# First adjacency pass in five sets of blocks, weighted one-hots on ScalarE, all duplicate counts in pass zero of a four-layer graph network

## The chip, the cores and the metric

One core of one Trainium2 chip runs the whole kernel in one launch. The metric is the device time in microseconds, the median of several runs.

## The reference, cut to what matters

A graph of 6250 nodes and 106250 directed edges (100000 and a self loop per node), sorted by destination. Four residual layers, each on `relu(layernorm(x))`:

```python
edge_index = stack([src, dst])                     # 106250 edges, sorted by dst
h = relu(layernorm(x))
# L0: an edge MLP gives each edge a weight; GCN with these weights
w = sigmoid(gelu(concat(h[src], h[dst]) @ mlp_w1 + mlp_b1) @ mlp_w2 + mlp_b2)
deg = segment_sum(w with loops of 1, dst); dinv = rsqrt(deg)
x = x + segment_sum((h @ conv_w)[src] * (dinv[src] * w * dinv[dst]), dst) + conv_b
# L1: two plain GCNs (128 -> 256 -> 128), with relu
# L2: message MLP, segment_sum(m[src], dst), update MLP on concat(h, agg)
# L3: three plain GCNs of 128 x 128
```

The sums over edges of L1 to L3 need only how often each pair (src, dst) occurs; those of L0 need a weight per edge.

## The kernel before

**Preparation.** Edges are cut into 831 tiles of 128. Nodes are cut into 49 windows (as destinations; `DB` = 49) and 49 chunks (as sources) of 128. Because a tile may span two windows, the edge passes walk over 880 steps, 220 groups (`GROUPS`) of four (`S` = 4).

**Pass zero** (the edge MLP). For each group POOL gathers four times 128 rows of `table` (`gather`, L569). SP copies the rows out to `h_rows` and loads what duplicate counting needs (`load_keys`, L398). TensorE spreads the destination half, VectorE adds the halves, ScalarE does Gelu and Tanh, and VectorE splits the new weights. VectorE also does the duplicate counts, `dedupe(n)` (L1083 to L1095): for four tiles of edges it counts how often the same (src, dst) stands in the tile and clears the place of all but one. There are 208 of them (`SCATTERS`), 146 (`EARLY`) in pass zero and 62 in pass one, as `counted(p, g)` hands them out.

**Scatters.** `adj` in HBM is the matrix of counts, f16, one block of 128 destinations by 49 x 128 sources for each window. Once POOL has issued all gathers and the blocks are zeroed, it issues 208 x 4 indirect DMAs that add counts to `adj` (`scatter`, L577). Tiles are cut into runs; the four tiles of a group come from four different runs, so that no two transfers under way touch one destination. A destination that two neighbouring runs share goes to a row of a spare block for the later run. The matrix thus has spare blocks, whose product is added to each block by a small one-hot matmul (`add_spare`, L838).

**Pass one** (the weighted sum of L0), while the scatters run. VectorE turns the low source bits into one-hots (`turn_low`, L1161), TensorE spreads the inverse degrees, VectorE picks them (`pick`, L1169), makes `norm` (L1174), writes weighted one-hots (L1192) and adds the products of TensorE (L801) to `acc` (L1189), the last two in `weigh_and_add`. A dense stage CONV0 of ten chunks follows.

**Six dense passes** over the adjacency blocks. A pass is one spare block and 49 blocks; each is 49 matmuls of 128 x 384 (`add_sources`, L830), and behind each go the steps of the layer (L850, L861, L870) and the spare's share (L838). In the first pass there are two sets of blocks, 0 to 35 and 36 to 48, each led by a spare block of its own. Set one may start when the scatters that concern it have landed (`needed`, worked out from the data in batches of four runs), set two when all have.

SP loads the blocks as halves of 25 and 24 chunks in a ring of five buffers (`AR` = 5), in the order written out in `halves_in`; half n of the first pass is half n mod 2 of unit n // 2. For each it waits until half n - 5 is used. Two more waits touch the change: the half that would overwrite a second spare half waits until POOL has added this to the first spare block in HBM,

```python
if n - AR in SECOND_SPARE:
    sp.wait_ge(combined[SECOND_SPARE.index(n - AR)], 16)
```

and so does the first spare load of the second pass. POOL issues this addition (L592) in its own order, behind all its scatters:

```python
for g in range(SCATTERS):
    scatter(g)
pool.wait_ge(half_used, 2)
for half, n in enumerate(SECOND_SPARE):
    ...
    nc.gpsimd.dma_start(adj_rows[SPARE, ...], halves[:, n % AR, ...], accum_op=ALU.add, ...)
```

Of the kernel before, what the change touches and what calls it, by code (L numbers as in the profile page):

```python
# [4 lines left out]
P = 128  # L5
# [35 lines left out]

SPARE = DB
BLOCKS = DB + 2
ROW_BITS, SRC_BITS = 13, 6
RUN = 2048
# [6 lines left out]

EARLY = GROUPS * 2 // 3
# [8 lines left out]
SETS = ((0, 36), (36, DB))  # L62
# [3 lines left out]
BATCH_SHIFT = 6  # L66
# [32 lines left out]
def build(nc, a, out):  # L99
# [12 lines left out]
    with ExitStack() as ctx, ExitStack() as early:  # L112
# [10 lines left out]
        needed = sb("needed", [P, 1], i32)  # L123
# [54 lines left out]
        in_first = sb("in_first", [P, TC + 1], f32, early)  # L178
# [14 lines left out]
        with ExitStack() as first:  # L193
            step_iota = sb("step_iota", [P, KPAD], f32, first)
            window_f = sb("window_f", [P, KPAD], f32, first)
            rows_n = sb("rows_n", [P, 2, TC, P], f32, first)
            src_nat = sb("src_nat", [P, KPAD], f32, first)
            dst_nat = sb("dst_nat", [P, KPAD], f32, first)
            changed = sb("changed", [P, KPAD], bf16, first)
            carried = sb("carried", [P, SLOTS * RUN_TILES], f32, first)  # L200
            late = sb("late", [P, SLOTS], f32, first)
            spare_row = sb("spare_row", [P, SLOTS, RUN_TILES], f32, first)
            place_n = sb("place_n", [P, KPAD], i32, first)
# [6 lines left out]
        with ExitStack() as turned:  # L210
            rows = sb("rows", [P, RING, S, D], f32, turned)
            onehot = sb("onehot", [P, SUMS, S, P], f32, turned)
            low_row = sb("low_row", [P, LOW, S * P], bf16, turned)
            low_t = sb("low_t", [P, 2, S, P], bf16, turned)
            inv_all = sb("inv_all", [P, S, PARTS, DB], f32, turned)
            inv_src = sb("inv_src", [P, 2, S], f32, turned)
            norm = sb("norm", [P, 2, S], f32, turned)
# [47 lines left out]
        ps_needed = ps[:, 7 * BANK + P + 1:7 * BANK + P + 2]  # L265
# [56 lines left out]
        in_first_set = sem("in_first_set")  # L322
        combined = [sem(f"combined{half}") for half in range(2)]
# [27 lines left out]
        picked = sem("picked")  # L351
        degrees_set = sem("degrees_set")
# [63 lines left out]
        SECOND_SPARE = [half_number(UNITS.index((0, SPARE + 1)), half) for half in range(2)]  # L416
# [14 lines left out]
        def _(sp):  # L431
# [34 lines left out]
            for n in range(counted(0, 2).stop):  # L466
                load_keys(sp, n)
            sp.wait_ge(zero_set, 1)
            for g in range(GROUPS):
                rows_gathered(sp, g)  # L470
                sp.dma_start(h_rows[g].rearrange("p (s d) -> p s d", s=S), rows_0[:, g % RING, :, MH:MH + D]).then_inc(rows_kept[g % RING], 16)
                for n in counted(0, g + 3) if g + 3 < GROUPS else ():
# [19 lines left out]
            for n, u, half in halves_in:  # L492
                q, w = UNITS[u]
                if (q, w, half) == (0, SPARE + 1, 0):
                    for s in range(S):
                        sp.wait_ge(scattered[s], 16 * SCATTERS)
                elif (q, w, half) == (0, SPARE, 0):
                    sp.wait_ge(needed_set, 1)
                    at_least = sp.value_load(needed[0:1, 0:1], min_val=16 * RUN_TILES, max_val=16 * SCATTERS)
                    for s in range(S):  # L500
                        sp.wait_ge(scattered[s], at_least)
                c0, c1 = HALVES[half]
                after(sp, half_used, n - AR + 1)
                if n - AR in SECOND_SPARE:
                    sp.wait_ge(combined[SECOND_SPARE.index(n - AR)], 16)
                if (q, w) == (1, SPARE):
                    sp.wait_ge(combined[half], 16)
                sp.dma_start(halves[:, n % AR, 0:c1 - c0, :].rearrange("p c j -> p (c j)"),
                             adj_rows[w, :, c0 * P:c1 * P]).then_inc(half_in[n % AR], 16)
                if q == LAYERS - 1 and half == 1 and 5 <= w < DB:  # L510
                    b = w - 5
                    sp.wait_ge(out_set, b + 1)
                    sp.dma_start(out[b * P:(b + 1) * P, :], x[:, b, :]).then_inc(out_stored, 16)
# [10 lines left out]
        def _(pool):  # L524
# [64 lines left out]
            for half, n in enumerate(SECOND_SPARE):  # L589
                c0, c1 = HALVES[half]  # L590
                pool.wait_ge(half_in[n % AR], 16 * (n // AR + 1))
                nc.gpsimd.dma_start(adj_rows[SPARE, :, c0 * P:c1 * P],  # L592
                                    halves[:, n % AR, 0:c1 - c0, :].rearrange("p c j -> p (c j)"),
                                    accum_op=ALU.add, max_dma_last_dim=4096).then_inc(combined[half], 16)

        @block.scalar
        def _(act):
# [98 lines left out]
        def _(pe):  # L696
# [12 lines left out]
            pe.wait_ge(in_first_set, 1)  # L709
            nc.tensor.matmul(ps_needed, ones[:, :], in_first[:, TC:TC + 1], start=True, stop=True).then_inc(needed_counted, 1)  # L710
# [196 lines left out]
        def _(dve):  # L907
# [27 lines left out]
            link(nc.vector.tensor_scalar(in_first[:, 0:TC], last_window[:, :], float(SETS[0][1]), None, ALU.is_lt))  # L935
            nc.vector.tensor_reduce(in_first[:, TC:TC + 1], in_first[:, 0:TC], AX.X, ALU.add).then_inc(in_first_set, 1)
# [22 lines left out]
            link(nc.vector.tensor_scalar(late[:, :], ps_carry_b, float(P * SETS[0][1]), float(P), ALU.is_ge, ALU.mult))  # L959
            link(nc.vector.tensor_tensor(spare_row[:, :, :], spare_row[:, :, :], late[:, :].unsqueeze(2).to_broadcast([P, SLOTS, RUN_TILES]), ALU.add))  # L960
# [203 lines left out]
            def pick(g):  # L1164
# [9 lines left out]
                nc.vector.tensor_tensor(norm[:, j, :], inv_src[:, j, :], weight[:, g * S:(g + 1) * S], ALU.mult).then_inc(picked, 1)  # L1174
                dve.wait_ge(picked, g + 1)


            def weigh_and_add(g):
                behind = g - SUMS + 2
                if behind >= 0:  # L1180
                    window = windows(behind, ENG.DVE)
                    dve.wait_ge(summed, GROUPS + behind + 1)
                if g < GROUPS:
                    after(dve, summed, GROUPS + g - SUMS + 1 if g >= SUMS else 0)
                for s in range(S):
                    if behind >= 0:
                        after(dve, added, behind * S + s)
                        to = acc[:, bass.ds(window[s], 1), :].rearrange("p o d -> p (o d)")
                        nc.vector.tensor_tensor(to, to, products[:, behind % SUMS, s, :], ALU.add).then_inc(added, 1)  # L1189
                    if g < GROUPS:  # L1190
                        k = g * S + s
                        last = nc.vector.tensor_scalar(onehot[:, g % SUMS, s, :], window_iota[:, :], local_dst[:, k:k + 1],  # L1192
                                                       norm[:, g % 2, s:s + 1], ALU.is_equal, ALU.mult)
                if g < GROUPS:
                    last.then_inc(onehots, 1)
                    for n in counted(1, g):
                        dedupe(n)

            for g in range(GROUPS + SUMS):
                if g < GROUPS:  # L1200
                    turn_low(g)
                if 0 < g <= GROUPS:
                    pick(g - 1)
                if 0 < g < GROUPS + SUMS - 1:
                    weigh_and_add(g - 1)
# [142 lines left out]
```

## Time and profile before

| | us |
|---|---|
| median of 3 runs | 5242.03 (5237.89 to 5245.15) |
| profiled execution, its time | 5242.9 |
| profiled execution, its span | 5241.1 |
| TensorE matmul busy | 3938.7 |
| VectorE busy | 2852.4 |
| GpSimd busy | 2187.0 |
| ScalarE busy | 496.3 |

The stages in the trace: preparation and the edge MLP's tables to 213.5 us (first gather); pass zero to 1327.6 (first scatter); pass one to about 2395; CONV0 to 2552.4; six dense passes to the end; the last scatter is issued at 2893.8. In the rows, a line such as L577 is a line of the kernel. "Idle before" and "waited for" give what released an engine; "issue" is time in which the profile shows nothing that it waited for.

### The profile page before, as it was taken

To read this page: it belongs to the slowest core of one execution; us is meant where nothing else is said; L and a number is where in the kernel's file an instruction comes from. 1 tells how busy PE (TensorE), PEld (TensorE's weight loads), DVE (VectorE), ACT (ScalarE), POOL (GpSimd) and SP (SyncE) were. 2 spreads that over 40 slices of the span, in tenths; PEclk is the share of its full clock that TensorE was granted. 3 is DMA by queue.
4 is the path that set the end of the run, shared out by engine and by line. 5 is a ranking of instruction groups with operands and counts; after the bars stand their busy time and mean duration, and the time that the engine had idled before them with its cause. 6 is when DMAs were issued, how large, how long until landed. Compare 5 with 4: busy or idle time off the path is not lost.

```text
span 5241.1 us, 76944 instructions
## 1 busy us (share of the span) xinstructions
PE 3938.7 (75%) x24567; PEld 2745.0 (52%) x24567; DVE 2852.4 (54%) x13130; ACT 496.3 (9%) x1390; POOL 2187.0 (42%) x1748
## 2 busy tenths in 40 slices
PE   3355555555455555553699999999999999999999
PEld 3333334433444444442466566666666666666666
DVE  4677777777888888887422244444443333333111
ACT  0122222222000000000000011111110000000000
POOL 2277777777888888888888100000000000000000
PEclk7555555555555555555799999999999999999999
DMA  2387778777555555552576655555555666666665
GB/s 71 114 249 241 248 240 248 242 246 206 117 99 98 99 100 99 100 95 10 117 175 164 186 178 178 179 173 167 167 168 182 190 192 191 191 190 192 198 199 168
DMA packets 498766, 873.85 MB, mean 167 GB/s; under 512 B 168988, under 2 KB 343660, under 8 KB 491852
## 3 DMA queue, kind: packets, MB, share of 16 engines
q1 hardware_dynamic: 321868, 761.54, 46.6%
q0 software_dynamic: 163040, 89.35, 12.0%
q10 hardware_dynamic: 13472, 18.03, 1.5%
q8 instruction: 215, 3.52, 0.3%
q14 instruction: 171, 1.40, 0.1%
HBM read 717.58 MB, written 151.13 MB: 166 GB/s over the span
## 4 chain that ended last, share of the span: by engine, by line
PE 46%; POOL 24%; DVE 14%; issue 10%; DMA 5%; DVEq 1%; SPq 0%; ACT 0%; POOLq 0%; ACTq 0%
PE ps L830 40%; POOL rows L569 14%; POOL adj L577 10%; DVE inv_all L1169 4%; DVE acc L1189 3%; DMA rows<-table,src_of 2%; DVE onehot L1192 2%; PE ps L861 1%; DMA adj<-count,place 1%; DVEq L405 1%; PE ps L870 1%; DVE same L1083 1%; DVE low_t L1161 1%; PE ps L838 1%; DMA h_rows<-rows 1%
## 5 line engine op out<-in xcount | busy, mean ns | idle before, releaser
L830 PE MATMUL ps<-parts,halves 128*128 128x384 bf16 x14749 | 2509.9, 326 | 29.5 <-DVE parts L1233 19.0
L830 PEld LDWEIGHTS ps<-parts,halves 128*128 128x128 f16 x14749 | 1445.0, 98 | 924.6 <-DVE parts L1233 19.1
L577 POOL DMA_INDIRECT adj<-count,place x832 | 1312.1, 1577 | 256.0 <-issue 243.6
L569 POOL DMA_INDIRECT rows<-table,src_of x880 | 845.9, 961 | 398.6 <-issue 256.5
L1256 DVE TENSOR_REDUCE summed_f<-ps 128x128 f32<-128x384 f32 x252 | 140.6, 558 | 1411.1 <-PE ps L838 1386.1
L792 PE MATMUL ps<-inv_parts,low_t 128*128 128x147 bf16 x880 | 148.1, 323 | 506.9 <-DVE low_t L1161 506.9
L770 PE MATMUL ps<-dst_mlp,onehot_t 128*128 x2640 | 364.7, 232 | 155.9 <-DVE pre L1110 74.3
L801 PE MATMUL ps<-rows,onehot 128*128 128x128 f32 x1760 | 440.8, 432 | 3.2 <-DVE onehot L1192 3.2
L801 PEld LDWEIGHTS ps<-rows,onehot 128*128 128x128 f32 x1760 | 402.7, 334 | 3.8 <-DVE onehot L1192 3.8
L770 PEld LDWEIGHTS ps<-dst_mlp,onehot_t 128*128 128x128 bf16 x2640 | 274.5, 104 | 236.1 <-issue 178.1
L792 PEld LDWEIGHTS ps<-inv_parts,low_t 128*128 128x128 bf16 x880 | 83.0, 130 | 570.8 <-DVE low_t L1161 559.5
L784 PE MATMUL ps<-weight_parts,onehot_b 128*128 128x4 bf16 x880 | 132.2, 184 | 292.7 <-DVE weight_parts L1133 278.1
L1189 DVE TENSOR_TENSOR acc<-acc,ps 128x128 f32 x880 | 256.3, 291 | 143.1 <-DVE norm L1174 139.6
L1192 DVE TENSOR_SCALAR onehot<-window_iota,local_dst,norm 128x128 f32<-128x128 f32 x880 | 329.1, 393 | 0.6
L784 PEld LDWEIGHTS ps<-weight_parts,onehot_b 128*128 128x128 bf16 x880 | 91.4, 104 | 371.1 <-issue 348.6
L1169 DVE SCALAR_TENSOR_TENSOR inv_all<-chunk_iota,chunk_of,ps 128x147 f32<-128x147 f32 x880 | 269.0, 362 | 0.6 <-PE ps L792 0.6
L1083 DVE SCALAR_TENSOR_TENSOR same<-key_row,key,first_weight 128x128 bf16<-128x128 f32 x832 | 244.0, 350 | 30.3 <-DMA key_row<-key_list 29.8
L670 ACT COPY source_t<-ps 128x128 f32<-128x128 f32 x196 | 52.2, 266 | 1523.1 <-PE ps L850 1523.1
L1110 DVE TENSOR_TENSOR pre<-ps,rows 128x256 f32<-128x256 f32 x220 | 92.1, 419 | 189.2 <-DMA rows<-table,src_of 184.7
L761 PE MATMUL ps<-ident_b,onehot_b 128*128 128x128 bf16 x880 | 129.9, 302 | 63.4 <-DVE onehot_b L1101 62.5
L1101 DVE TENSOR_SCALAR onehot_b<-window_iota_b,local_dst 128x128 bf16<-128x128 bf16 x880 | 167.1, 274 | 0.0
L630 ACT COPY onehot_t<-ps 128x512 bf16<-128x512 bf16 x220 | 129.0, 587 | 394.4 <-PE ps L761 388.9
(222 smaller groups left out, 3278.2 us busy)
## 6 DMA issues: line engine op xcount, KB each, us to landing
halves<-adj SPq DMA_DIRECT2D x301, 800.0 KB, 4.4
halves<-adj SPq DMA_DIRECT2D x301, 768.0 KB, 4.4
adj<-slot_of SPq DMA_DIRECT2D x51, 1568.0 KB
h_rows<-rows SPq DMA_DIRECT2D x220, 256.0 KB
rows<-h_rows SPq DMA_DIRECT2D x220, 256.0 KB, 3.9
key_row<-key_list SPq DMA_DIRECT2D x146, 256.0 KB, 5.2
low_row<-low_list SPq DMA_DIRECT2D x220, 128.0 KB, 3.6
key_row<-key_list ACTq DMA_DIRECT2D x62, 256.0 KB, 3.8
```

Source lines behind the costliest of these rows:

```text
L569: nc.gpsimd.indirect_dma_start(out=rows_0[:, g % RING, s, :], out_offset=None, in_=table[:, :], in_offset=bass.IndirectOffsetOnAxis(ap=src ...
L577: nc.gpsimd.indirect_dma_start(out=adj[:, :], out_offset=bass.IndirectOffsetOnAxis(ap=place[:, k:k + 1], axis=0), in_=count16[:, k:k + 1], ...
L770: last = nc.tensor.matmul(ps_mlp[:, g % 2, s, :], onehot_t[:, g % 2, s, :], dst_mlp[:, bass.ds(window[s], 1), part, :].rearrange("p o m -> ...
L784: last = nc.tensor.matmul(ps_deg[:, bass.ds(window[s] * (PARTS + 1), PARTS + 1)], onehot_b[:, g % HELD, s, :], weight_parts[:, g % 2, s, : ...
L792: last = nc.tensor.matmul(ps_inv[:, g % 2, s // 2, s % 2, :, :].rearrange("p t c -> p (t c)"), low_t[:, g % 2, s, :], inv_parts[:, :, :].r ...
L801: last = nc.tensor.matmul(products[:, g % SUMS, s, :], onehot[:, g % SUMS, s, :], rows[:, g % RING, s, :], start=True, stop=True)
L830: last = nc.tensor.matmul(ps_sum[u % 3], halves[:, n % AR, c - HALF_C * (c >= HALF_C), :], parts[q % 2][:, c, :, :].rearrange("p t d -> p ...
L1083: last = nc.vector.scalar_tensor_tensor(same[:, s, :], key_row[:, n % KEYS, s, :], key[:, n * S + s:n * S + s + 1], first_weight[:, :], AL ...
L1101: last = nc.vector.tensor_scalar(onehot_b[:, g % HELD, s, :], window_iota_b[:, :], local_dst[:, k:k + 1], None, ALU.is_equal)
L1169: last = nc.vector.scalar_tensor_tensor(inv_all[:, s, :, :], chunk_iota[:, :, :], chunk_of[:, k:k + 1], ps_inv[:, j, s // 2, s % 2, :, :], ...
L1189: nc.vector.tensor_tensor(to, to, products[:, behind % SUMS, s, :], ALU.add).then_inc(added, 1)
L1192: last = nc.vector.tensor_scalar(onehot[:, g % SUMS, s, :], window_iota[:, :], local_dst[:, k:k + 1], norm[:, g % 2, s:s + 1], ALU.is_equa ...
```

## The change

It does three things.

1. **Weighted one-hots of pass one on ScalarE.** The tensor_scalar of L1192 (is_equal, then times `norm`) goes from VectorE. ScalarE takes `Abs(local_dst - iota)` into a new buffer `distance` and then `Relu(norm - 4 * distance)` into `onehot`, two instructions for each of the 880 steps. `norm` gets four buffers in place of two. The adds to `acc` become a loop of their own, with the loading of the windows ahead of `turn_low`.
2. **All 208 duplicate counts in pass zero.** `counted(g)` spreads them over the 220 groups; all `load_keys` go from SP.
3. **Five sets in the first dense pass**: 0 to 27, 28 to 37, 38 to 43, 44 to 46, 47 and 48, each with a spare block. Runs are half as long (1024 edges, 8 tiles), so there are 103 shared places in place of 51, and the batches of `needed` are half as large. 54 blocks are zeroed in place of 51. Each of the four later spare blocks is added in HBM to the first, in two halves.

```diff
+NORMS = 4
+SETS = ((0, 28), (28, 38), (38, 44), (44, 47), (47, DB))
+EARLIER = len(SETS) - 1
-BLOCKS = DB + 2
+BLOCKS = DB + len(SETS)
-RUN = 2048
+RUN = 1024
-EARLY = GROUPS * 2 // 3
-SETS = ((0, 36), (36, DB))
-BATCH_SHIFT = 6
+BATCH_SHIFT = 5
...
-        def counted(p, g):
-            first, many = (0, EARLY) if p == 0 else (EARLY, SCATTERS - EARLY)
-            return range(first + many * g // GROUPS, first + many * (g + 1) // GROUPS)
+        def counted(g):
+            return range(SCATTERS * g // GROUPS, SCATTERS * (g + 1) // GROUPS)
...
-        SECOND_SPARE = [half_number(UNITS.index((0, SPARE + 1)), half) for half in range(2)]
+        SPARE_HALVES = {half_number(UNITS.index((0, SPARE + n)), half): (n - 1, half) for n in range(1, len(SETS)) for half in range(2)}
...
-                if (q, w, half) == (0, SPARE + 1, 0):
+                if (q, w, half) == (0, SPARE + EARLIER, 0):
                     for s in range(S):
                         sp.wait_ge(scattered[s], 16 * SCATTERS)
-                elif (q, w, half) == (0, SPARE, 0):
+                elif q == 0 and w >= SPARE and half == 0:
                     sp.wait_ge(needed_set, 1)
-                    at_least = sp.value_load(needed[0:1, 0:1], ...)
+                    at_least = sp.value_load(needed[0:1, w - SPARE:w - SPARE + 1], ...)
...
                 after(sp, half_used, n - AR + 1)
-                if n - AR in SECOND_SPARE:
-                    sp.wait_ge(combined[SECOND_SPARE.index(n - AR)], 16)
                 if (q, w) == (1, SPARE):
-                    sp.wait_ge(combined[half], 16)
+                    sp.wait_ge(combined[EARLIER - 1][half], 16)
+                if n - AR in SPARE_HALVES:
+                    k, its = SPARE_HALVES[n - AR]
+                    sp.wait_ge(combined[k][its], 16)
...
             pool.wait_ge(half_used, 2)
-            for half, n in enumerate(SECOND_SPARE):
+            for n, (k, half) in SPARE_HALVES.items():
                 c0, c1 = HALVES[half]
                 pool.wait_ge(half_in[n % AR], 16 * (n // AR + 1))
+                if k > 0:
+                    pool.wait_ge(combined[k - 1][half], 16)
                 nc.gpsimd.dma_start(adj_rows[SPARE, :, c0 * P:c1 * P],
...
-            for g in range(GROUPS):
-                for n in counted(1, g):
-                    load_keys(act, n)
+            def measure(g):
+                after(act, onehots, GROUPS + g - 1 if g > 1 else 0)
+                for s in range(S):
+                    k = g * S + s
+                    last = nc.scalar.activation(distance[:, g % 2, s, :], window_iota[:, :], ACT.Abs, bias=local_dst[:, k:k + 1], scale=-1.0)
+                last.then_inc(measured, 1)
+            def weigh(g):
+                act.wait_ge(picked, g + 1)
+                act.wait_ge(measured, g + 1)
+                after(act, summed, GROUPS + g - SUMS + 1 if g >= SUMS else 0)
+                for s in range(S):
+                    last = nc.scalar.activation(onehot[:, g % SUMS, s, :], distance[:, g % 2, s, :], ACT.Relu, bias=norm[:, g % NORMS, s:s + 1],
+                                                scale=-4.0)
+                last.then_inc(onehots, 1)
+            act.wait_ge(inverses_split, 1)
+            pipeline(GROUPS, [(0, measure), (1, weigh)])
...
-            link(nc.vector.tensor_scalar(late[:, :], ps_carry_b, float(P * SETS[0][1]), float(P), ALU.is_ge, ALU.mult))
-            link(nc.vector.tensor_tensor(spare_row[:, :, :], spare_row[:, :, :], late[:, :].unsqueeze(2).to_broadcast([P, SLOTS, RUN_TILES]), ALU.add))
+            for n in range(EARLIER):
+                link(nc.vector.tensor_scalar(late[:, n, :], ps_carry_b, float(P * SETS[n][1]), float(P), ALU.is_ge, ALU.mult))
+                link(nc.vector.tensor_tensor(spare_row[:, :, :], spare_row[:, :, :],
+                                             late[:, n, :].unsqueeze(2).to_broadcast([P, SLOTS, RUN_TILES]), ALU.add))
...
-                for n in counted(0, g):
+                for n in counted(g):
                     dedupe(n)
...
-                        last = nc.vector.tensor_scalar(onehot[:, g % SUMS, s, :], window_iota[:, :], local_dst[:, k:k + 1],
-                                                       norm[:, g % 2, s:s + 1], ALU.is_equal, ALU.mult)
-                    for n in counted(1, g):
-                        dedupe(n)
```

## Rows read from the trace of the kernel before

**Rows 1.** Windows: busy us (instructions) of PE, PEld, DVE, ACT, POOL; granted clock, DMA share, GB/s.

```profile
600.00:1000.00 400.00, 220.12 (x1590) 159.57 (x1589) 302.82 (x1703) 99.47 (x237) 304.02 (x316) 0.50 0.79 245
...
1600.00:1800.00 200.00, 103.89 (x504) 91.62 (x504) 170.09 (x907) 0.00 (x0) 167.41 (x108) 0.50 0.56 99
...
2600.00:3000.00 400.00, 389.50 (x2501) 255.78 (x2499) 108.78 (x339) 36.85 (x124) 249.73 (x161) 0.98 0.69 176
```

**Rows 2.** POOL's two lines: duration in ns min/median/max, first and last start.

```profile
L569 POOL DMA_INDIRECT rows<-table,src_of x880: 942/946/1158, 213.5 to 1326.3; - x176
...
L577 POOL DMA_INDIRECT adj<-count,place x832: 1555/1561/6774, 1327.5 to 2893.8; - x167
```

**Rows 3.** Timeline around the last scatter: start, us, instruction, idle before and releaser.

```profile
2890.51 0.33 PE L838 MATMUL ps<-spare_parts,slot_of 128*128 128x384 bf16 x1
...
2893.76 1.58 POOL L577 DMA_INDIRECT adj<-count,place  x1 [0.30 <-issue]
2896.97 92.52 SPq L508 DMA_DIRECT2D halves<-adj  x24
...
2901.34 5.45 PE L830 MATMUL ps<-parts,halves 128*128 128x384 bf16 x17 [10.50 <-DMA halves<-adj]
...
2901.85 1.29 POOL L592 DMA_DIRECT2D adj<-halves  x1 [6.50 <-DMA halves<-adj]
```

**Rows 4.** Timeline of PE at the start of the dense passes.

```profile
2552.38 19.01 PE L830 MATMUL ps<-parts,halves 128*128 128x384 bf16 x98 [18.95 <-DVE parts L1233]
```

**Rows 5.** The chain that ended last, from 2912 to 3031: start, us, what.

```profile
2912.98 7.96 PE ps L830 x49
...
2921.11 2.76 PE ps L830 x17
...
2930.23 2.76 PE ps L830 x17
...
3030.42 0.16 PE ps L838
```

**Rows 6.** DMA issues: KB each, us from issue to landing.

```profile
halves<-adj SPq DMA_DIRECT2D x301, 800.0 KB, 4.4
...
adj<-halves POOLq DMA_DIRECT2D x1, 800.0 KB, 12.1
adj<-halves POOLq DMA_DIRECT2D x1, 768.0 KB, 15.2
```

**Rows 7.** Timeline of VectorE in the preparation.

```profile
72.44 0.20 DVE L959 TENSOR_SCALAR late<-ps 128x51 f32<-128x51 f32 x1
...
73.71 1.01 DVE L961 TENSOR_TENSOR spare_row<-spare_row,dst_nat 128x816 f32<-128x816 f32 x1
```

**Rows 8.** Timeline of VectorE in pass zero: where three groups' weight steps begin.

```profile
803.53 0.28 DVE L1123 TENSOR_SCALAR new_weight<-tanh_half 128x4 f32<-128x4 f32 x1
...
808.24 0.16 DVE L1123 TENSOR_SCALAR new_weight<-tanh_half 128x4 f32<-128x4 f32 x1
...
811.11 0.24 DVE L1123 TENSOR_SCALAR new_weight<-tanh_half 128x4 f32<-128x4 f32 x1
```

**Rows 9.** Waits in pass zero (213 to 1327): total us, times, longest us.

```profile
DVE pre L1110 <- DMA rows<-table,src_of: 182.2, 78, 8.4
...
DVE same L1083 <- DMA key_row<-key_list: 29.8, 21, 2.2
```

**Rows 10.** DMA queue of SP: packets, MB, share of 16 engines over the span.

```profile
q1 hardware_dynamic: 321868, 761.54, 46.6%
```

**Rows 11.** Timeline of VectorE in pass one: begin and end of a group without a count.

```profile
1705.13 0.42 DVE L1161 TENSOR_SCALAR low_t<-low_row,tile_iota 128x512 bf16<-128x512 bf16 x1
...
1709.35 0.35 DVE L1161 TENSOR_SCALAR low_t<-low_row,tile_iota 128x512 bf16<-128x512 bf16 x1
```

**Rows 12.** Timeline of ScalarE in the first dense pass: its nearest instructions.

```profile
2906.93 0.27 ACT L670 COPY source_t<-ps 128x128 f32<-128x128 f32 x1 [18.48 <-PE ps L850]
...
2910.14 0.63 ACT L677 ACTIVATE hidden<-ps,b_L_gnn_b 128x128 f32<-128x128 f32 x2 [2.94 <-PE ps L861]
```

More of the change, by code:

```diff
@@ L122, in build @@
         place = sb("place", [P, KPAD], i32)
[L123 removed]
+        needed = sb("needed", [P, EARLIER], i32)
         count16 = sb("count16", [P, KPAD], f16)
@@ L177, in build @@
         shift = sb("shift", [P, P], f32, early)
-        in_first = sb("in_first", [P, TC + 1], f32, early)
+        in_sets = sb("in_sets", [P, EARLIER, TC], f32, early)
+        in_sets_p = sb("in_sets_p", [P, EARLIER], f32, early)
         upto = sb("upto", [P, P], bf16, early)
@@ L200, in build @@
             carried = sb("carried", [P, SLOTS * RUN_TILES], f32, first)
-            late = sb("late", [P, SLOTS], f32, first)
+            late = sb("late", [P, EARLIER, SLOTS], f32, first)
             spare_row = sb("spare_row", [P, SLOTS, RUN_TILES], f32, first)
@@ L320, in build @@
         degree_roots = sem("degree_roots")
-        in_first_set = sem("in_first_set")
-        combined = [sem(f"combined{half}") for half in range(2)]
+        in_sets_set = sem("in_sets_set")
+        combined = [[sem(f"combined{n}_{half}") for half in range(2)] for n in range(EARLIER)]
         needed_counted = sem("needed_counted")
@@ L351, in build @@
         picked = sem("picked")
+        measured = sem("measured")
         degrees_set = sem("degrees_set")
@@ L465, in _ @@
             sp.wait_ge(keys_stored, 16)
-            for n in range(counted(0, 2).stop):
+            for n in range(counted(2).stop):
                 load_keys(sp, n)
@@ L471, in _ @@
                 sp.dma_start(h_rows[g].rearrange("p (s d) -> p s d", s=S), rows_0[:, g % RING, :, MH:MH + D]).then_inc(rows_kept[g % RING], 16)
-                for n in counted(0, g + 3) if g + 3 < GROUPS else ():
+                for n in counted(g + 3) if g + 3 < GROUPS else ():
                     load_keys(sp, n)
@@ L588, in _ @@
             pool.wait_ge(half_used, 2)
-            for half, n in enumerate(SECOND_SPARE):
+            for n, (k, half) in SPARE_HALVES.items():
                 c0, c1 = HALVES[half]
                 pool.wait_ge(half_in[n % AR], 16 * (n // AR + 1))
+                if k > 0:
+                    pool.wait_ge(combined[k - 1][half], 16)
                 nc.gpsimd.dma_start(adj_rows[SPARE, :, c0 * P:c1 * P],
                                     halves[:, n % AR, 0:c1 - c0, :].rearrange("p c j -> p (c j)"),
-                                    accum_op=ALU.add, max_dma_last_dim=4096).then_inc(combined[half], 16)
+                                    accum_op=ALU.add, max_dma_last_dim=4096).then_inc(combined[k][half], 16)
         @block.scalar
@@ L708, in _ @@
             last.then_inc(tiles_counted, 1)
-            pe.wait_ge(in_first_set, 1)
-            nc.tensor.matmul(ps_needed, ones[:, :], in_first[:, TC:TC + 1], start=True, stop=True).then_inc(needed_counted, 1)
+            pe.wait_ge(in_sets_set, 1)
+            nc.tensor.matmul(ps_needed, ones[:, :], in_sets_p[:, :], start=True, stop=True).then_inc(needed_counted, 1)
             pe.wait_ge(rows_n_set, 1)
@@ L933, in _ @@
             last.then_inc(reached_set, 1)
-            link(nc.vector.tensor_scalar(in_first[:, 0:TC], last_window[:, :], float(SETS[0][1]), None, ALU.is_lt))
-            nc.vector.tensor_reduce(in_first[:, TC:TC + 1], in_first[:, 0:TC], AX.X, ALU.add).then_inc(in_first_set, 1)
+            for n in range(EARLIER):
+                last = nc.vector.tensor_scalar(in_sets[:, n, :], last_window[:, :], float(SETS[n][1]), None, ALU.is_lt)
+            link(last)
+            nc.vector.tensor_reduce(in_sets_p[:, :], in_sets[:, :, :], AX.X, ALU.add).then_inc(in_sets_set, 1)
             dve.wait_ge(needed_counted, 1)
@@ L1173, in pick, with add_products @@
                 dve.wait_ge(picking, g + 1)
[L1174 to L1184, printed above, removed]
-                for s in range(S):
[L1186 to L1191, printed above, removed]
-                        last = nc.vector.tensor_scalar(onehot[:, g % SUMS, s, :], window_iota[:, :], local_dst[:, k:k + 1],
-                                                       norm[:, g % 2, s:s + 1], ALU.is_equal, ALU.mult)
-                if g < GROUPS:
-                    last.then_inc(onehots, 1)
-                    for n in counted(1, g):
-                        dedupe(n)
+                after(dve, onehots, GROUPS + g - NORMS + 1 if g >= NORMS else 0)
+                nc.vector.tensor_tensor(norm[:, g % NORMS, :], inv_src[:, j, :], weight[:, g * S:(g + 1) * S], ALU.mult).then_inc(picked, 1)
+            def add_products(g, window):
+                dve.wait_ge(summed, GROUPS + g + 1)
+                for s in range(S):
+                    after(dve, added, g * S + s)
+                    to = acc[:, bass.ds(window[s], 1), :].rearrange("p o d -> p (o d)")
+                    nc.vector.tensor_tensor(to, to, products[:, g % SUMS, s, :], ALU.add).then_inc(added, 1)
             for g in range(GROUPS + SUMS):
+                window = windows(g - SUMS, ENG.DVE) if g >= SUMS else None
                 if g < GROUPS:
@@ L1203, in _ @@
                     pick(g - 1)
-                if 0 < g < GROUPS + SUMS - 1:
-                    weigh_and_add(g - 1)
+                if window:
+                    add_products(g - SUMS, window)
             dve.wait_ge(added, GROUPS * S)
```

8 lines of the change are left out of this document (5 added, 3 removed).

## The prediction, on record before the change was run

> **What bounds the kernel now.** I read the stages first, then what each waits for at its end, then the chain that ended last. The windows by stage [rows 1] show pass zero with POOL and VectorE each 76% busy, pass one with VectorE 85%, and the dense passes with TensorE 97% and more at the full 2.4 GHz (both edge passes have the granted clock at 0.50, 1.2 GHz).
>
> POOL runs without a break from the first gather to the last scatter [rows 2]. Its gathers take (1326.3 - 213.5) / 879 = 1.266 us each, 5.06 us a group; its scatters (2893.8 - 1327.5) / 831 = 1.885 us each, 7.54 us a group. The pace of the scatters is the same beside pass one and beside the dense passes (108 in 200 us, 161 in about 300 us), so neither work slows it.
>
> Two chains then meet [rows 3]. TensorE ends set one at 2890.8, 338 us after it began at 2552.4 [rows 4]. The last scatter is issued at 2893.8, lands by 2897.0, SP loads the second spare's half, TensorE goes on at 2901.3 after only 10.5 us of idle time. From there it does 14 units to 3030.6 [rows 5], and then the five other passes, which take the remaining 5241.1 - 3030.6 = 2210.5 us. So a gain needs less work behind the last scatter: the start of the dense passes and the end of POOL bind almost equally, and only both together can be moved.
>
> **What the change wants.** With the last set only three units long (a spare and blocks 47, 48), the first pass could end some 100 us earlier. This holds if TensorE can do the 51 other units before 2901. I look at what stands in the way.
>
> **The wait that I expect to decide.** Spare n leads its set at unit 29, 40, 47 or 51; the second spare's halves are thus numbers 58 and 59. With five buffers, half 63 (the second half of unit 31) overwrites half 58, and SP waits for `combined[0][0]` before it issues it. That addition is POOL's, and POOL's program order has it behind all 832 scatters. Before, this wait had no price of its own, since the only such spare was loaded after the last scatter anyway. Now its set is ready after 168 groups of scatters: windows up to 37 are 38 x 128 x 17 edges / 128 = 646 tiles, so 20 full batches of 32 and one more, 21 x 8 = 168. That is 1327.5 + 672 x 1.885 = 2594, 300 us before POOL is through. Behind the waiting SP stand all further loads, and TensorE waits for them. TensorE gets through units 29 and 30 and 25 columns of unit 31, and then stands, however early it began. It is there in time if the dense passes begin before 2912 - 31.5 x 9.12 = 2625, and even today's start, 2552, does that.
>
> The sum, from the last scatter:
> - POOL issues the first addition at 2893.8 + 1.6 + 0.3 = 2895.7. It lands 12.1 us later [rows 6]: 2907.8. This row was taken beside five loads; alone it could be as short as a plain load of this size, 4.4; the other half's 15.2 is the upper end. I take 12.1, as the row of the same operation and size.
> - Half 63 lands 4.4 us behind its issue: TensorE resumes at 2912.2, 10.9 us after its resumption of today.
> - Work left: 24 columns of unit 31, with their layer steps, 24 x 0.162 (7.96 / 49) = 3.9, and the 1.0 of layer steps and share of the spare that stand there, 4.9; eight blocks of 9.12 (2930.23 - 2921.11 [rows 5]) = 73.0. Then three sets. A spare unit has no share of the spare to add (8.96) and the block behind it no layer steps (8.13, as 2921.11 - 2912.98), the rest 9.12: 8.96 + 8.13 + 5 x 9.12 = 62.7, then 35.3, then 26.2. Together 202.1. The first 17 columns after the pause run cold, as today (5.45 us [rows 3] against 2.76 [rows 5]): + 2.7.
> - First pass ends at 2912.2 + 204.8 = 3117.0 against 3030.6: **+86.4 us**.
>
> The second addition (768 KB, 15.2 us) lands at about 2912.5 and half 64 by 2917, while TensorE is busy with half 63 until 2919. The later additions are hidden: a spare half is loaded five halves ahead, so 2.5 units or 22.8 us pass from its issue to the end of its use; load and addition take 4.4 + 12.1 = 16.5 or 4.4 + 15.2 = 19.6. If that cover were gone, the four halves still in the ring, 18 us, are a second one.
>
> The Trainium skill ("DMA: Bandwidth & Descriptors", "Anatomy of one DMA — SWDGE (gpsimd) path") fits such a transfer as 2.0 us plus its bytes over 436 GB/s; for 800 KB I work out an estimate of 3.9 us, where the row has 12.1. By it the sum would be 8 us less. The same page's section "SWDGE vs HWDGE vs iDMA" says that only GpSimd can issue a DMA that accumulates, which speaks against this change: the addition can't go to an idle queue, it has to share POOL's order with the scatters. That no trace here shows by itself; the trace shows only that it stands there.
>
> **Preparation.** Three more pairs of `late` and `spare_row`, each 73.71 - 72.44 = 1.27 us [rows 7], in a stretch where VectorE has no gap, ahead of everything: 3 x 1.27 = **+3.8 us**. The rest (three comparisons for `in_sets`) lies beside TensorE's counting. Bounds: 0 if waits behind it take it up, 5 with the longer tiny operations.
>
> **Pass zero, 62 more counts.** A group with a count keeps VectorE 808.24 - 803.53 = 4.71 us, one without 2.87 [rows 8]: 1.84 us a count, 114 us in all, against 182.2 us that VectorE waits for gathers [rows 9]. Even a group with a count is shorter than POOL's 5.06. So POOL stays the bound and this costs nothing; the six-deep ring of rows takes up single delays. The key loads, 62 x 0.262 = 16 MB, and three more zeroed blocks, 5 MB: at 761.54 MB in 46.6% of the span [rows 10], 312 GB/s for all engines busy, they are 67 us of all DMA engines in 1113, so the share goes from 0.79 [rows 1] to 0.85. That is still no bound, but loads land later, and each count may wait as 21 of 146 do today (29.8 us in all [rows 9]). The last zeroing goes out at group 212, some 35 us before the first scatter. I take 0 for all of it, with 15 us as the upper end; below nothing it can't be, since POOL's own pace is the bound.
>
> **Pass one.** VectorE's group is 4.22 us [rows 11]. Of its 14 instructions it loses four, and the 62 counts go. In proportion that is 3.0 us; if the adds, now without one-hots between them, wait for each other, up to 4.2. I take 3.5, 770 us in place of 1056. ScalarE does eight instructions of 0.27 to 0.32 us [rows 12], 2.1 to 2.6 us a group, less than VectorE. With 157 us from the end of pass one to the first dense matmul as today, TensorE begins at about 2270, at the latest at 2552 if nothing is gained. All of this gain, 280 us, is paid back standing at half 63, and a bad guess here changes nothing: worth **0**.
>
> The sum: 86.4 + 3.8 = 90.2. The profiled execution has a span of 5241.1 and a time of 5242.9, 0.9 over the median of the runs. 5242.0 + 90.2 = **5332 us**, 1.7% slower.
>
> **Rivals.**
> - *The wait does not bind, and the last set is the bound.* Speaks for it: the scatters for all sets are in time (by the same count 120, 168, 192 and 200 groups), and nothing else waits. Then TensorE begins unit 51 at 2901.3 + 3.8 and ends the pass 26.2 + 2.7 us later, at 2934.0, 96.6 before today: 5145. It needs TensorE at work by 2901 - 51 x 9.1 = 2437 and the first addition done by about 2620, when half 63 is due; against it stands POOL's order, in which that comes at 2895 at the earliest. Chance 0.05.
> - *Pass zero becomes bound by VectorE or by DMA.* Each group would then be over 5.06, and all scatters shift with it. VectorE has 0.35 us to spare in a group with a count; with 0.1 to 0.2 us more than that, from later key rows, 20 to 40 us come on top: 5352 to 5372. Against it stand 182 us of spare time. Chance 0.10.
> - *The later additions are not hidden.* If two halves of one spare took over 40 us, each of sets three to five would stand some 5 to 10 us, the second pass's first load too: 5345 to 5370. Chance 0.06.
> - *ScalarE makes pass one so slow that the dense start decides*: only beyond 2625, so from (2625 - 157 - 1339) / 220 = 5.1 us a group on, twice what the rows give. Chance 0.02.
> - *No change*: only if savings and the stall cancel; no row gives it. Chance 0.02.
>
> **Numbers.** My forecast holds 0.75: 5332, its own range 5320 (addition 4.4, no price in preparation) to 5350 (15.2, and 15 us in pass zero). With the two slower rivals half in, 5318 to 5362 leaves less than 2 in 10 out. 0.2% of 5242 is 10 us, about what a measurement of this kernel can tell from no change. Faster 0.05, same 0.02, slower 0.93.
>
> **What would show it.** A TensorE gap of about 290 us, from about 2620 to 2912, ended by a half's load; SP's longest wait on an addition; the first addition right behind the last scatter, at about 2900; first scatter at 1331; pass one's end near 2115; the second pass's first block at about 3121. The prediction is wrong if the half behind the second spare is loaded before the last scatter, if the first scatter comes after 1345, or if there are further gaps before 3120.

## The result, and the profile after

The changed kernel takes **5319.3 us** (median, 5317.8 to 5323.9), against 5243.0 before: ratio 1.015, 95% interval 1.0139 to 1.0162. The forecast was 5332, with 5318 to 5362 as its range. The profiled execution has a span of 5318.4 us, against 5241.1. (Lines have moved: the scatter is L580, the addition of spares L597, `add_sources` L852.)

The page of the changed kernel, busy time and slices of 133 us:

```profile
PE 3964.7 (75%) x24714; PEld 2761.0 (52%) x24714; DVE 2736.9 (51%) x12276; ACT 1064.6 (20%) x3150; POOL 2181.6 (41%) x1754
...
PE   4355555555566666369601999999999999999999
```

TensorE does only 26 us more work. But its row has a hole: it falls to 0 and 1 behind a stretch of 9, 6. The windows of the changed kernel (columns as [rows 1]) show the hole, and that pass one now has ScalarE at work and TensorE two thirds busy:

```profile
600.00:1000.00 400.00, 219.59 (x1583) 158.79 (x1580) 343.29 (x2004) 102.78 (x238) 303.44 (x318) 0.50 0.83 259
1600.00:1700.00 100.00, 66.51 (x324) 58.88 (x324) 80.83 (x378) 68.61 (x216) 83.83 (x54) 0.50 0.55 107
2650.00:2700.00 50.00, 0.00 (x0) 0.00 (x0) 0.00 (x0) 0.00 (x0) 41.77 (x28) 0.50 0.22 0
```

From 2650 to 2700 only POOL works. The waits of SP's queue over the whole span say on what:

```profile
SPq L510 <- DMA adj<-halves: 306.3, 2, 303.0
...
SPq L503 <- DMA adj<-count,place: 89.1, 3, 61.9
```

L510 is the wait for `combined` before a spare's buffer is loaded anew, 303.0 us at one time. TensorE's timeline, POOL's timeline and the chain that ended last, of the changed kernel, show how the wait begins and ends:

```profile
2324.46 5.82 PE L852 MATMUL ps<-parts,halves 128*128 128x384 bf16 x25 [17.95 <-DVE parts L1245]
...
2596.54 5.01 PE L852 MATMUL ps<-parts,halves 128*128 128x384 bf16 x17 [7.92 <-DMA halves<-adj]
...
2615.70 2.93 PE L852 MATMUL ps<-parts,halves 128*128 128x384 bf16 x17
2618.47 0.27 PE L872 MATMUL ps<-ident,source 128*128 128x128 f32 x1
2618.57 1.46 PE L852 MATMUL ps<-parts,halves 128*128 128x384 bf16 x8
...
2903.20 3.06 PE L852 MATMUL ps<-parts,halves 128*128 128x384 bf16 x9 [283.16 <-DMA halves<-adj]
```

```profile
2888.28 1.55 POOL L580 DMA_INDIRECT adj<-count,place  x1 [0.31 <-issue]
2889.26 3.15 POOL L597 DMA_DIRECT2D adj<-halves  x2
2969.39 1.19 POOL L597 DMA_DIRECT2D adj<-halves  x1 [76.98 <-DMA halves<-adj]
```

```profile
2889.26 8.27 DMA adj<-halves
...
2897.60 5.55 DMA halves<-adj
...
2903.20 3.06 PE ps L852 x9
...
3107.70 0.16 PE ps L860
```

The reader is to see three things. TensorE stops after 17 + 8 = 25 columns of a block, just the first half of unit 31, and then stands 283.2 us (the 7.9 us at 2596.5 are the wait for the scatters of the second set). The last scatter is issued at 2888.3, and only behind it comes the first addition, 8.3 us long; the load behind it ends the wait. The first pass then ends at 3107.9, against 3030.6 before [rows 5]: + 77.3 us, which is the difference of the spans, 5318.4 - 5241.1. The other five passes take 2210.5 us in both.

What the change was to bring did come: dense passes begin at 2324.5 in place of 2552.4 [rows 4], 228 us earlier. All of it, and 77 us more, went into the two waits of 7.9 and 283.2 us and the three more units.

### The profile page after: what moved, and what is told of

Same layout as the page of the kernel before. It is cut to its first block, busy times and chain, and to the rows that moved or that the text cites. A ratio compares the mean times of both kernels' runs of the same rounds, so it can differ in the third digit from the quotient of the medians.

```text
span 5318.4 us, 78624 instructions
## 1 busy us (share of the span) xinstructions
PE 3964.7 (75%) x24714; PEld 2761.0 (52%) x24714; DVE 2736.9 (51%) x12276; ACT 1064.6 (20%) x3150; POOL 2181.6 (41%) x1754
## 4 chain that ended last, share of the span: by engine, by line
PE 47%; POOL 34%; issue 11%; DMA 5%; DVE 2%; SPq 0%; ACT 0%; POOLq 0%; DVEq 0%; ACTq 0%
PE ps L852 41%; POOL adj L580 22%; POOL rows L572 13%; DMA rows<-table,src_of 2%; PE ps L883 1%; DMA h_rows<-rows 1%; DMA adj<-count,place 1%; PE ps L892 1%; PE ps L860 1%; PE ps L895 1%; PE ps L872 0%; PE ps L773 0%; PE ps L728 0%; DVE chunk L1060 0%; PE ps L724 0%
## 5 line engine op out<-in xcount | busy, mean ns | idle before, releaser
L852 PE MATMUL ps<-parts,halves 128*128 128x384 bf16 x14896 | 2534.6, 326 | 309.0 <-DMA halves<-adj 291.1
L852 PEld LDWEIGHTS ps<-parts,halves 128*128 128x128 f16 x14896 | 1459.5, 98 | 1213.7 <-DMA halves<-adj 291.8
L580 POOL DMA_INDIRECT adj<-count,place x832 | 1302.5, 1566 | 257.0 <-issue 249.7
L668 ACT ACTIVATE onehot<-distance,norm 128x128 f32<-128x128 f32 x880 | 280.9, 390 | 249.8 <-DVE norm L1201 249.8
L660 ACT ACTIVATE distance<-window_iota,local_dst 128x128 f32<-128x128 f32 x880 | 280.9, 390 | 9.2 <-DVE inv_parts L1180 2.2
L766 PE MATMUL ps<-ident,chunk 128*128 128x128 f32 x100 | 26.5, 430 | 183.9 <-DVE chunk L1228 107.9
```

What stands on the lines that cost most here:

```text
L580: nc.gpsimd.indirect_dma_start(out=adj[:, :], out_offset=bass.IndirectOffsetOnAxis(ap=place[:, k:k + 1], axis=0), in_=count16[:, k:k + 1], ...
L660: last = nc.scalar.activation(distance[:, g % 2, s, :], window_iota[:, :], ACT.Abs, bias=local_dst[:, k:k + 1], scale=-1.0)
L668: last = nc.scalar.activation(onehot[:, g % SUMS, s, :], distance[:, g % 2, s, :], ACT.Relu, bias=norm[:, g % NORMS, s:s + 1], scale=-4.0)
L852: last = nc.tensor.matmul(ps_sum[u % 3], halves[:, n % AR, c - HALF_C * (c >= HALF_C), :], parts[q % 2][:, c, :, :].rearrange("p t d -> p ...
```

## The experiments

Each ratio is to the kernel before on the same chip at the same time. The first four kernels ran on a chip where that takes 5240.6 us; the others on one where it takes 5514 to 5516; pass zero is longer there (last section). So times of the two groups are compared by ratio, or by stretches inside a trace.

**1. The addition without the ring.** The later spares are added from HBM to HBM, so no buffer waits for an addition; POOL issues them between scatters, two groups after those that concern the spare:

```diff
-                if n - AR in SPARE_HALVES:
-                    k, its = SPARE_HALVES[n - AR]
-                    sp.wait_ge(combined[k][its], 16)
...
+COMBINE_AFTER = (168, 192, 200, 208)
...
             for g in range(SCATTERS):
                 scatter(g)
+                for k in range(EARLIER):
+                    if g == min(COMBINE_AFTER[k] + 2, SCATTERS - 1):
+                        combine(k)   # adj_rows[SPARE] += adj_rows[SPARE + 1 + k]
```

> The changed kernel, but each later spare block is added to the first from HBM to HBM by POOL, two scatter groups after the groups that concern it (168, 192, 200, 208), so that no buffer of the ring waits for an addition. Theory (the ring's wait on POOL's order is the whole loss): no TensorE gap of 283 us; last set starts at about 2898 plus 8 us for six additions issued between scatters, first pass ends near 2935, time 5138 to 5150, against 5319 of the change and 5243 before. Rival (the loss is in the three more units, in 62 more counts or in more DMA traffic): those are all still there, so 5310 or more stays.

Measured: 5166.0 us, ratio 0.9857 (0.9840 to 0.9873): 153 us less than the change, and 1.4% less than before. The rival is out: without the wait the loss is gone, with the units, the counts and the traffic still there. The time is 16 us over the top of what I expected, and POOL's timeline of hbm_add shows why:

```profile
2614.42 3.06 POOL L594 DMA_DIRECT2D adj<-adj  x2
2617.78 1.66 POOL L578 DMA_INDIRECT adj<-count,place  x1 [0.31 <-issue]
...
2634.13 1.55 POOL L578 DMA_INDIRECT adj<-count,place  x1 [9.12 <-DMA adj<-count,place]
```

The four scatters behind the additions are issued at once, but the next waits 9.12 us for one of them to land. The DMA issues of hbm_add from 2612 to 2640 show that the second half of the addition lands 17.5 us behind its issue; SP issues seven loads of halves in the same stretch:

```profile
adj<-adj POOLq DMA_DIRECT2D x1, 800.0 KB, 10.8
adj<-adj POOLq DMA_DIRECT2D x1, 768.0 KB, 17.5
```

The last scatter starts at 2919.0, 31 us after the change's 2888.3. The Trainium skill ("DMA: Bandwidth & Descriptors", "SWDGE vs HWDGE vs iDMA") says that only one queue is allocated to GpSimd's software path. This wait agrees with that, though no run here separates the queue from the memory.

**2. Two sets again**, all else as in the change:

```diff
-SETS = ((0, 28), (28, 38), (38, 44), (44, 47), (47, DB))
+SETS = ((0, 36), (36, DB))
```

> The changed kernel with the two sets of before (0 to 35, 36 to 48): one-hots on ScalarE, all counts in pass zero and the shorter runs stay. Theory: the first set may start after 160 groups, so dense passes begin near 2540 and set two at 2896: 5236 to 5242, about as before. Rival (counts in pass zero or the smaller runs cost): first scatter some 10 us or more later than before's 1327.6, and over 5250.

Measured: 5235.4 us, ratio 0.9990 (0.9980 to 1.0000). With two sets, the first two parts of the change together cost nothing and bring next to nothing: TensorE waits 228.9 us for 160 groups of scatters before it begins, at 2533.2. The first scatter stands at 1325.6, 2 us before that of the kernel before [rows 2], so 62 more counts in pass zero cost nothing on this chip.

**3. Five sets alone**, on the kernel before: one-hots on VectorE and 62 counts in pass one.

```diff
 (kernel before)
-SETS = ((0, 36), (36, DB))
+SETS = ((0, 28), (28, 38), (38, 44), (44, 47), (47, DB))
-RUN = 2048
+RUN = 1024
 ... and what goes with them: needed, late, spare_row, combined
```

> The kernel before with the five sets and shorter runs alone: one-hots on VectorE, 62 counts in pass one. Theory: dense passes begin at about 2556 in place of 2298, but TensorE stands at half 63 until the first addition all the same, so the time is that of the change, 5319 to 5330, with a gap of only some 60 us in place of 283. Rival (loss from the other two parts): about 5243.

Measured: 5323.4 us, ratio 1.0156 (1.0139 to 1.0173), the change's loss in full. Dense passes begin at 2551.4, 227 us later than in the change, and the time is the same. TensorE's timeline of five_sets_only:

```profile
2908.46 3.06 PE L835 MATMUL ps<-parts,halves 128*128 128x384 bf16 x9 [71.94 <-DMA halves<-adj]
```

The hole is 71.9 us in place of 283.2. How long TensorE stands doesn't matter here; when it resumes, and with how many units left, decides.

**4. The second spare later.** Four sets, so that unit 37 has the first later spare, in place of 29, and 13.5 units are left behind the wait in place of 22.5:

```diff
-SETS = ((0, 28), (28, 38), (38, 44), (44, 47), (47, DB))
+SETS = ((0, 36), (36, 44), (44, 47), (47, DB))
```

> The changed kernel with four sets, 0 to 35, 36 to 43, 44 to 46, 47 and 48: the first later spare stands at unit 37 in place of 29. Theory: TensorE begins at about 2540 (160 groups), comes to the waiting half (39.5 units) at about 2901, about when the addition is done, and has 13.5 units left in place of 22.5: first pass ends near 3024, time about 5236. Rival (each more unit costs its 8.6 us, two more than before): 5260.

Measured: 5237.8 us, ratio 0.9995 (0.9986 to 1.0005). TensorE's timeline of late_second_set:

```profile
2888.55 1.46 PE L852 MATMUL ps<-parts,halves 128*128 128x384 bf16 x8
2898.54 3.06 PE L852 MATMUL ps<-parts,halves 128*128 128x384 bf16 x9 [8.53 <-DMA halves<-adj]
```

It stops again after the 25th column, two units behind the spare, and resumes 15.3 us behind the last scatter's start (2883.3), as in the change (2903.2 - 2888.3 = 14.9). With nine units less behind the wait, 82 us are gone.

**5. A ring of four halves:**

```diff
-AR = 5
+AR = 4
```

> The changed kernel with a ring of four halves in place of five. Theory: the half that overwrites the spare's first half is 62 in place of 63, so TensorE stands 25 columns earlier and has those 25 columns (4.2 us) more to do behind the first addition: 5323 to 5324, the gap longer by the same 4 us. Rival (the stall has nothing to do with the ring's length, only the landed scatters matter): 5319, or, if four buffers are too few to hide loads, far more.

Measured: 5595.3 us, ratio 1.0148 (1.0131 to 1.0165). The 4 us can't be seen in a ratio with an interval of 19 us, but they are in the trace. TensorE's timeline of ring4:

```profile
2892.65 8.13 PE L852 MATMUL ps<-parts,halves 128*128 128x384 bf16 x49
2900.61 0.33 PE L860 MATMUL ps<-spare_parts,slot_of 128*128 128x384 bf16 x1
...
3174.22 5.45 PE L852 MATMUL ps<-parts,halves 128*128 128x384 bf16 x17 [273.29 <-DMA halves<-adj]
```

It stops a half earlier, after the whole of unit 30. From the last scatter's start (3159.3) to the end of the first pass (3383.2) it takes 224.0 us, in the change 3107.9 - 2888.3 = 219.6: 4.4 us more, where 4.2 was expected. So the wait stands where the ring meets the spare.

**6. All additions behind the last scatter**, HBM to HBM. This needs no constants from the data:

```diff
             for g in range(SCATTERS):
                 scatter(g)
+            for k in range(EARLIER):
+                combine(k)
```

> As hbm_add, but all eight additions from HBM to HBM are issued behind the last scatter, so that no scatter stands behind one. Theory: the last scatter is back at about 2886 to 2889 (2919 in hbm_add); the first pass ends near 2924; then the second pass's spare waits for a chain of four additions of 11 to 18 us, so TensorE stands 20 to 40 us at the pass boundary: 5155 to 5175. Rival (additions under way do not delay the scatters): last scatter still near 2919 and over 5180.

Measured: 5434.8 us, ratio 0.9861 (0.9844 to 0.9877), as good as the first. The scatters take 3159.4 - 1597.5 = 1561.9 us, against 1587.4 in hbm_add, so additions under way did delay them. In return TensorE now stands at the pass boundary. Its timeline in hbm_add_end:

```profile
3194.39 0.33 PE L859 MATMUL ps<-spare_parts,slot_of 128*128 128x384 bf16 x1
3214.82 4.25 PE L851 MATMUL ps<-parts,halves 128*128 128x384 bf16 x17 [20.10 <-DMA halves<-adj]
```

**7. No addition at all:** as 6, with `combine` and the second pass's wait left out.

> As hbm_add_end with no addition of the spare blocks at all: passes two to six leave the edges of the later spare blocks out of their sums. It shows what the additions themselves cost. Theory: last set starts at about 2895, first pass ends at about 2922, no gap at the boundary: 5132 to 5138. Rival (five sets carry a cost of their own beyond the wait): over 5150.

Measured: 5415.9 us, ratio 0.9825 (0.9809 to 0.9842). The additions cost 18.9 us, the 20.1 us of the boundary. (Between the two profiled spans it is only 14.0 us; no_add's last scatter starts 7.2 us later there, at 3166.6.) What this would be on the first chip can be worked out in two ways, both estimates. In ratio terms 0.9825 of 5240.6 is 5149. By the stretch from the start of the last scatter to the end it is less: 5412.8 - 3166.6 = 2246.2 us here, 5318.4 - 2888.3 = 2430.1 in the change, so 5319.3 - 183.9 = 5135. I had expected 5132 to 5138, and the rival "the last set is the bound" had 5145. So the change has a gain of about 94 to 106 us in it when spares cost nothing, and the wait turned it into a loss of 76.

**8. As 6, with the edge passes of before** (one-hots on VectorE, 62 counts in pass one):

> As hbm_add_end, but with one-hots on VectorE and 62 counts in pass one, as before. Theory: dense passes begin at about 2556 and TensorE has 54 units, about 489 us, without a stop: first pass ends near 3045, the additions are long done, and the time is 5250 to 5260, some 10 to 15 us over before; the other two parts of the change are then worth about 90 us. Rival (those two parts are worth nothing with the wait gone either): within 10 us of hbm_add_end.

Measured: 5538.7 us, ratio 1.0045 (1.0028 to 1.0062): 104 us over 6. TensorE begins at 2839.4 and never waits for a half. With the wait gone, five sets need the earlier start, and alone make the kernel slower. By the ratio it is 25 us, where I expected 10 to 15. The first pass takes 3327.6 - 2839.4 = 488.2 us, against 3030.6 - 2552.4 = 478.2 in the kernel before [rows 5], which contains 10.5 us of waiting for the last scatter. The three more units thus cost 20.5 us of work. From the first scatter to the first dense matmul it takes 1246.2 us here and 1223.3 in five_sets_only on the first chip, so the kernel before may well have no such wait on this chip, which would explain the other 10 us. It has no trace here, so this is not shown.

**9. One part of the two.** Base is 6, run once more. In counts_only the one-hots are back on VectorE; in onehots_only 62 counts are back in pass one.

> hbm_add_end once more, as the base for the two kernels beside it on the same chip. Theory: 1.4% under before; on a chip where pass zero ends near 1330, 5150 to 5165.

> As hbm_add_end, but with the weighted one-hots back on VectorE; all counts stay in pass zero. Theory: dense passes begin some 113 us (62 counts of 1.84) before those of the kernel before, at about 2440 in place of 2324; TensorE's 54 units then end near 2932, still ahead of the chain of additions that ends near 2946: within 5 us of hbm_add_end_b. Rival (each of the two parts is worth about half of what both are): 40 to 60 us over hbm_add_end_b.

> As hbm_add_end, but with 62 counts back in pass one; the one-hots stay on ScalarE. Theory: dense passes begin about 114 us later than in hbm_add_end, near 2438, and as in counts_only that still suffices: within 5 us of hbm_add_end_b. Rival (each part worth about half): 40 to 60 us over it.

Measured: 5433.2 us (0.9852, 0.9835 to 0.9870), 5436.3 (0.9860, 0.9842 to 0.9877) and 5425.3 (0.9836, 0.9818 to 0.9854). Either part alone does it: dense passes begin at 2618.5, 2733.7 and 2725.0, and the later start costs nothing: from 2600 to 3300 TensorE waits 107.5 us for halves in the first kernel, 2.2 and 0.6 in the other two. The third is 8 us under the first, 3 more than I expected; they are in the first scatter, 1600.4 against 1592.5. On this chip the 62 counts do lengthen pass zero a little: the first scatter comes at 1597.5 to 1603.6 in the five kernels that have them there, at 1592.5 and 1593.2 in the two that don't. onehots_only has the lowest ratio of the kernels that compute everything, but its interval overlaps that of its base.

A longer ring, which would move the wait to a later unit, was not run.

## Why the prediction was right, step by step

**The deciding wait.** Right: half 63, 25 columns into unit 31, released by the first addition behind the last scatter. The forecast's "however early it began" is experiment 3, its "two units behind the spare" experiments 4 and 5, and that nothing else loses time experiments 1 and 7.

**The sum.** Forecast + 90.2, measured + 76.3 (77.3 between the two profiled spans). Against the traces:

| term | forecast | measured |
|---|---|---|
| start of the last scatter, against before | + 3.8 | - 5.5 |
| from there to the issue of the addition | 1.9 | 1.0 |
| landing of the addition | 12.1 | 8.3 |
| from there to TensorE | 4.4 | 5.7 |
| work left in the first pass | 204.8 | 204.7 |
| other five passes | 2210.5 | 2210.5 |

The work of 22.5 units, made of four kinds of unit from [rows 5], is right to 0.1 us. The mis-sized term is POOL: I held its scatters to today's pace. They took 2888.3 - 1330.6 = 1557.7 us, against 1566.3 [rows 2], 8.6 less. That accounts for most of the 13 us. The addition was 3.8 us shorter than its term, and the load behind it 5.55 us in place of 4.4. The row of the kernel after:

```profile
L580 POOL DMA_INDIRECT adj<-count,place x832: 1552/1553/6767, 1330.6 to 2888.3; - x167
```

Two things go with it. One is the program. The median of one scatter is 1553 or 1554 ns in the kernels with six or eight additions (five_sets_only, late_second_set, hbm_add, ring4 and the rest) and 1561 in those with two or none (before, two_sets, no_add), wherever the one-hots are made. What in the program does it stays open. But it isn't the larger part: five_sets_only, with 1553, needs 1564.7 us for its scatters, only 1.6 less than before.

The other is where pass one makes its one-hots. two_sets has the median of 1561 but the one-hots on ScalarE, and needs 1559.1 us, 7.2 less than before. In POOL's timelines, from the start of the 21st scatter to that of the 421st, all in pass one, a scatter takes on average

| one-hots on | us |
|---|---|
| VectorE | 1.874 before, 1.871 five_sets_only, 1.869 counts_only |
| ScalarE | 1.864 two_sets, 1.858 the change, 1.858 hbm_add_end_b, 1.858 onehots_only |

hbm_add_end_b, counts_only and onehots_only differ in nothing else on one chip: counts in pass one leave the 1.858 as it is, one-hots on VectorE raise it to 1.869. The step that failed is thus my "neither work slows it". I had compared counts of scatters in 200 us (108), which can't tell 1.874 from 1.858. By what path VectorE's one-hots slow POOL, no run here shows.

**The addition's price.** 8.3 us, between the bounds of 4.4 and 12.1. The row that I took [rows 6] was measured beside five loads. The Trainium skill's fit for such a transfer ("DMA: Bandwidth & Descriptors", "Anatomy of one DMA — SWDGE (gpsimd) path") gives 3.9 us as an estimate; the trace has twice that, with SP's loads held up and only the last scatters and the second addition beside it, and decides.

**Preparation.** First scatter + 3.1 us, for 3.8, but that the sum fits is partly luck. The first gather starts 5.8 us later (219.3, against 213.5 [rows 2]), over my upper bound of 5, and the gathers then take 2.7 us less. The three more pairs themselves cost about what I had: 4.2 us in five_sets_only (end of the `dst_nat` step at 80.97, against 76.81 before), where the first gather starts at 216.5. It lies between 215.9 and 220.3 in all kernels with five sets, so single executions differ by as much as the term.

**Pass zero.** Right: 62 counts cost nothing on that chip. VectorE's wait for gathers fell from 182.2 us [rows 9] to 88.2, and POOL's gathers took 1110.1 us, against 1112.8. I had written that it can't be less than nothing; it was 2.7 us less, and why stays open. Waits of the changed kernel from 219 to 1329:

```profile
DVE pre L1136 <- DMA rows<-table,src_of: 88.2, 53, 6.4
DVE same L1109 <- DMA key_row<-key_list: 13.0, 23, 2.0
```

Later key rows, which I feared, did not come: their waits fell from 29.8 to 13.0 us. The DMA share rose to 0.83, for 0.85 forecast.

**Pass one.** 3.7 us a group (the adds run from 1357.6 to 2166.4; the group at 1600 takes 3.79), for 3.5. The adds, now without one-hots between them, follow each other at a distance. VectorE's timeline:

```profile
1606.17 1.58 DVE L1208 TENSOR_TENSOR acc<-acc,ps 128x128 f32 x4
1607.95 0.57 DVE L1187 TENSOR_SCALAR low_t<-low_row,tile_iota 128x512 bf16<-128x512 bf16 x1 [0.20 <-issue]
```

One add takes 0.29 us, so four of them leave about 0.4 us idle between them, and 0.20 us come ahead of `turn_low`. ScalarE's 1760 instructions keep it busy 0.32 us each (280.9 us for each 880), the upper end of [rows 12], no bound. Dense passes began at 2324, not 2270. As forecast, it changed nothing.

**Later additions.** Hidden, as forecast: TensorE's chain has no further gap to 3107.9.

**The rivals.** The one on the other side had its size about right: 5145, for 5135 to 5149 estimated from experiment 7. For that the ring must not wait and the spares must cost nothing; where the ring doesn't wait but the spares are added, the nearest measured on the first chip is 5166.0 (experiment 1).

## What to carry to other kernels

Before work is cut into more stages, read for every buffer that a stage uses who frees it, and what stands ahead of that instruction on its queue. A wait that costs nothing because its release is early in fact (here: behind the last scatter, when the stage began there anyway) becomes the bound as soon as the stage begins sooner. And where an earlier start is won, ask what it meets next: here either of two parts sufficed, both together were paid back in a stall, and with two sets both together brought 5 us (5235.4 against 5240.6).

## What the runs showed of the hardware that I had not expected

**The second chip.** There the kernel before takes 5514 us in place of 5241. It has no trace there, but ring4 there and the change on the first chip differ only in the ring's length: pass zero takes 1600.0 - 217.1 = 1382.9 us against 1330.6 - 219.3 = 1111.3, nearly all of the difference of 276 us in time. In no_add it lasts from 215.9 to 1600.3 us. Single instructions are not slower (a `same` takes 344 ns on average, 348 in the change on the first chip), but VectorE waits long for its own semaphores. Waits of VectorE in no_add from 217 to 1590:

```profile
DVE rest L1150 <- DVE weight_parts L1148: 83.0, 91, 1.4
DVE place L1114 <- DVE count L1111: 63.7, 81, 1.1
DVE weight L1146 <- DVE new_weight L1144: 62.5, 79, 1.2
```

On the first chip none of these shows as a wait. A step that follows another by 0.20 us there, for instance, at times comes 0.7 us after it in no_add's timeline. POOL then waits 304.0 us for VectorE in no_add, where it waits 7.6 in the change on the first chip. So a chain of small steps with a semaphore each can set the time on one chip and be hidden on another. From the first scatter to the first dense matmul ring4 takes 1019.7 us, 26 more than the change; this is hidden behind the wait for POOL. Why the steps come late there, no run here shows.

**POOL's queue.** A scatter issued behind two additions of 0.8 MB landed so late that the next stood 9.1 us, where the others shown wait 0.3 us (experiment 1).
